# Handing more gathered columns of a graph network's edge passes to ScalarE, VectorE, SyncE and TensorE

## What is computed

```python
# a convolution layer
h = x @ W
msg = h[src] * norm[:, None]
out = segment_sum(msg, dst, num_segments=n_nodes)
# an edge convolution: theta, phi and a maximum
msg = (x[src] - x[dst]) @ tw.T + tb + phi[dst]
agg = segment_max(msg, dst, num_segments=n_nodes)
```

## Time and profile before

| | us |
|---|---|
| median of three runs | 9439.49 (9435.47 to 9441.98) |
| the profiled execution | 9444.14 |
| its span, first to last instruction | 9442.3 |
| a pass, first to last gather (passes 2 to 7) | 980.4 |
| the first pass | 1009.4 |

### The profile page before, as it was taken

One profiled execution on the slowest core, in us unless ns is written; L12 is line 12 of the kernel. 1 busy time (PEld: TensorE's weight loads), 2 busy tenths in 40 slices (PEclk: granted clock), 3 DMA queues, 4 the chain that ended last, 5 costly groups with the idle time before them and its releaser, 6 DMA issues. The chain is left out here.

```text
span 9442.3 us, 137452 instructions
## 1 busy us (share of the span) xinstructions
PE 1819.4 (19%) x9607; PEld 1531.1 (16%) x9607; DVE 3654.1 (39%) x20408; ACT 3485.0 (37%) x23810; POOL 6987.7 (74%) x6815
## 2 busy tenths in 40 slices
PE   2000057788884000020002000020002000020000
PEld 1000046777774000010001000010001000010000
DVE  4333344444443333333333333333334333333333
ACT  4444221111114444334442444334442444324441
POOL 5777668888883777777777777777776777777777
PEclk6555567777777555565556555565555555555555
DMA  6444535555553333333333333333334333333333
GB/s 214 161 159 158 190 79 77 77 77 77 75 72 111 108 108 112 110 108 108 113 111 111 111 109 108 113 105 112 108 110 138 103 117 111 109 108 110 108 112 128
DMA packets 483882, 1071.04 MB, mean 113 GB/s; under 512 B 162484, under 2 KB 293278, under 8 KB 428104
## 3 DMA queue, kind: packets, MB, share of 16 engines
q0 software_dynamic: 310432, 442.95, 21.5%
q1 hardware_dynamic: 169557, 619.06, 17.8%
q10 hardware_dynamic: 2940, 1.00, 0.1%
HBM read 511.83 MB, written 559.14 MB: 113 GB/s over the span
## 5 line engine op out<-in xcount | busy, mean ns | idle before, releaser
L1035 POOL DMA_INDIRECT WORK<-table,S x5502 | 5194.3, 944 | 1923.2 <-issue 1689.0
L1071 DVE COPY FE<-XF 128x4 uint8 x9856 | 1311.1, 190 | 3271.9 <-issue 1824.8
L1114 ACT COPY FE<-XF 128x4 uint8 x20608 | 2101.3, 191 | 1104.6 <-issue 1092.0
L1134 ACT COPY WORK<-psum 128x512 f32<-128x512 f32 (+1 forms) x1456 | 846.3, 581 | 2874.1 <-DVE psum L1089 2864.6
L1304 POOL DMA_INDIRECT acc<-TOT,stage x832 | 1301.3, 1564 | 274.6 <-issue 209.7
L1089 DVE SCALAR_TENSOR_TENSOR psum<-psum,RESET,WORK 128x128 f32<-128x128 f32 x3320 | 1189.1, 358 | 493.3 <-DMA WORK<-table,S 426.8
L1154 PE MATMUL psum<-ident,FE 128*128 128x128 f32 x238 | 106.5, 447 | 6110.0 <-ACT FE L1114 4714.0
L1089 DVE SCALAR_TENSOR_TENSOR psum<-psum,KEEP,WORK 128x128 f32<-128x128 f32 x2490 | 896.9, 360 | 639.9 <-DMA WORK<-table,S 278.8
L1154 PEld LDWEIGHTS psum<-ident,FE 128*128 128x128 f32 x238 | 43.3, 182 | 6172.5 <-issue 5903.0
L1438 ACT COPY TOT<-psum 128x512 f32<-128x512 f32 x208 | 121.9, 586 | 1250.2 <-DMA acc<-TOT,stage 1245.0
L1509 DVE SCALAR_TENSOR_TENSOR BASE<-psum,WEIGHT,BASE 128x128 f32<-128x128 f32 x832 | 234.1, 344 | 761.9 <-PE psum L1379 761.8
(11 more groups left out here) (255 smaller groups left out, 2540.4 us busy)
## 6 DMA issues: line engine op xcount, KB each, us to landing
run_rows<-WORK SPq DMA_DIRECT2D x357, 1024.0 KB, 4.2
WORK<-table SPq DMA_DIRECT2D x10752, 0.5 KB
WORK<-table,S POOLq DMA_INDIRECT x5502, 2.6
fill_rows<-BASE SPq DMA_DIRECT2D x52, 1024.0 KB, 6.8
WORK<-fill_rows SPq DMA_DIRECT2D x104, 512.0 KB, 3.7
table<-TF SPq DMA_DIRECT2D x56, 384.0 KB
WORK<-carry_rows SPq DMA_DIRECT2D x49, 384.0 KB, 6.6
acc<-TOT,stage POOLq DMA_INDIRECT x832, 3.3
```

The lines of the kernel that those rows point to most:

```text
L1035: pool.indirect_dma_start(RING_T[:, b * WIDE + k, :], None, table, table_row(table, INDEX[:, t:t + 1]))\
L1071: i = dve.tensor_copy(PICKED[:, s, e:e + 1].bitcast(u8), TT[:, ds(held_rows["dve"][e % 32], 4)])
L1114: i = act.copy(PICKED[:, j % 2, e:e + 1].bitcast(u8), TT[:, ds(held_rows["act"][e % 32], 4)])
L1134: act.copy(RING_T[:, t % SPAN:t % SPAN + n, :], CHAINED[:, t % PSUM_COLS:t % PSUM_COLS + n, :])\
```

## The change

46 columns of AWAY become 81: ScalarE 23 to 30, VectorE 11 to 24, SyncE 12 to 15, and TensorE, which brought none, 12. Copies are made in units of 32 edges, one register load each (UNIT, four units to a column). ScalarE does a unit at five of every eight groups of four columns, ahead of the lift; VectorE a unit at every other group; TensorE a unit at every fourth. TensorE's copy is a matmul with the identity as weights and one column of XF as moving data, into PSUM bank 7, which ScalarE copies to PICKED when all 128 edges are there (`drawn`). Tiles are turned three groups ahead of use in banks 5 and 6 and copied to the ring two groups ahead. The chain of running values has 20 columns of PSUM instead of 24. SyncE fetches the second to last column of every third (once in sixteen blocks: fourth) block: a half after store c-3 and one after store c-2, where it no longer waits for the store just issued. XF is read back after block 50. The place numbers for ROWB are made by 12 strided operations instead of 46.

```diff
-PSUM_COLS = 24
-BY_ACT = [t for t in range(60, 772, 32)]
-BY_DVE = [t for t in range(108, 772, 64)]
-BY_SP = [t for t in range(84, 800, 64)]
-EDGES = 16
-X_BLOCK = 48
-STEP_EDGES = 2
+PSUM_COLS = 20
+UNIT = 32
+UNITS = P // UNIT
+TT_LAST = 800
+ACT_QUADS = [q for q in range(TT_LAST // QUAD) if q % 8 in (0, 1, 3, 4, 6)]
+BY_ACT = [t for t in (QUAD * (q + 5) for q in ACT_QUADS[UNITS - 1::UNITS]) if t < TT_LAST]
+DVE_STEPS = list(range(4, TT_LAST, 8))
+BY_DVE = [t for t in (QUAD * (s // QUAD + 5) + 1 for s in DVE_STEPS[UNITS - 1::UNITS]) if t < TT_LAST]
+PE_QUADS = list(range(1, TT_LAST // QUAD, 4))
+BY_PE = [t for t in (QUAD * (q + 6) + 3 for q in PE_QUADS[UNITS - 1::UNITS]) if t < TT_LAST]
+SP_BLOCKS = [c for c in range(3, TT_LAST // WIDE) if c % 16 in (3, 6, 9, 12, 0)]
+BY_SP = [WIDE * c + WIDE - 2 for c in SP_BLOCKS]
+X_BLOCK = 50
...
                 def pick_edges(t):
+                    if t not in DVE_STEPS:
+                        return
+                    j, unit = divmod(DVE_STEPS.index(t), UNITS)
...
+                    if unit == 0:
+                        wait(dve, tt_copied, len(tt_quads) if j == 0 else 0)
+                        wait(dve, off_turned, FROM_TT.index(BY_DVE[j - 2]) + 1 if j > 1 else 0)
+                    rows = row_offsets(mybir.EngineType.DVE, len(BY_ACT) + j, unit)
+                    for e in range(UNIT):
+                        i = dve.tensor_copy(PICKED[:, 2 + j % 2, unit * UNIT + e:unit * UNIT + e + 1].bitcast(u8),
+                                            TT[:, ds(rows[e], 4)])
...
                 for q in range(quads):
                     pick_edges(q)
+                    for j, col in enumerate(BY_PE):
+                        if q == col // QUAD - 4:
+                            act.wait_ge(built_p, j + 1)
+                            wait(act, off_turned, FROM_TT.index(BY_PE[j - 2]) + 1 if j > 1 else 0)
+                            act.copy(PICKED[:, 4 + j % 2, :], bank(7)[:, 0:P]).then_inc(drawn, 1)
...
+                    rows = row_offsets(mybir.EngineType.PE, len(BY_ACT) + len(BY_DVE) + j, unit, 1)
+                    for e in range(UNIT):
+                        m = nc.tensor.matmul(bank(7)[:, unit * UNIT + e:unit * UNIT + e + 1], ident[:],
+                                             XF[:, ds(rows[e], 1)], start=True, stop=True)
...
+                for q in range(quads):
+                    for j, col in enumerate(FROM_TT):
+                        if q == col // QUAD - 3:
+                            turn(j, col)
+                    pick_edges(q)
...
                 def fetch(after):
                     for j, col in enumerate(BY_SP):
                         c = col // WIDE
-                        k = after - max(c - RING, -1)
-                        parts_of = ((0, 64), (64, 64)) if c >= RING else ((0, 128),)
-                        if not 0 <= k < len(parts_of):
+                        half = after - (c - RING + 1)
+                        if half not in (0, 1):
                             continue
...
+                        wait(sp, stored[c % RING], c // RING * 16 if half == 0 else 0)
+                        for unit in range(half * UNITS // 2, (half + 1) * UNITS // 2):
+                            rows = row_offsets(mybir.EngineType.SP, len(AWAY) - len(BY_SP) + j, unit, 4 * F)
+                            for e in range(UNIT):
+                                p = unit * UNIT + e
+                                sp.dma_start(RING_T[p:p + 1, col % SPAN, :].bitcast(u8),
+                                             flat_table[:, ds(rows[e], 4 * F)]).then_inc(fetched[j % 2], 16)
...
-                fetch(-1)
```

More of the change, by code:

```diff
@@ L632, in _ @@
                                   ALU.is_equal).then_inc(hot, 1)
-                for k, (t, size) in enumerate([(t, 4) for t in BY_ACT + BY_DVE] + [(t, 4 * F) for t in BY_SP]):
-                    i = dve.tensor_single_scalar(AWAY_F[:, k:k + 1], SRCF[:, t:t + 1], float(size), ALU.mult)
+                k = 0
+                for cols_of, period, size in ((BY_ACT, 5, 4), (BY_DVE, 1, 4), (BY_PE, 1, 1), (BY_SP, 5, 4 * F)):
+                    n = len(cols_of)
+                    for r in range(period):
+                        own = cols_of[r::period]
+                        assert own == list(range(own[0], own[-1] + 1, own[1] - own[0]))
+                        i = dve.tensor_single_scalar(AWAY_F[:, k + r:k + n:period],
+                                                     SRCF[:, own[0]:own[-1] + 1:own[1] - own[0]],
+                                                     float(size), ALU.mult)
+                    k += n
                 i.then_inc(hot, 1)
@@ L995, in _, with row_offsets @@
                 wait(sp, x_parked, 16 * NG if x_loads == 1 else 0)
-        def row_offsets(engine, k, first, n, size=4):
+        def row_offsets(engine, k, unit, size=4):
             return nc.values_load_multi_w_load_instructions(
-                ROWB[k:k + 1, first:first + n], engines=[engine], min_val=0, max_val=(N_PAD - 1) * size,
+                ROWB[k:k + 1, unit * UNIT:(unit + 1) * UNIT], engines=[engine], min_val=0,
+                max_val=(N_PAD - 1) * size,
                 skip_runtime_bounds_check_because="the offsets are made of node numbers below N_PAD")[1]
@@ L1059, in pick_edges @@
                 def pick_edges(t):
[L1060 to L1074, removed]
+                    if t not in DVE_STEPS:
+                        return
+                    j, unit = divmod(DVE_STEPS.index(t), UNITS)
+                    if j >= len(BY_DVE):
+                        return
+                    if unit == 0:
[5 more added lines that the diff above has]
+                                            TT[:, ds(rows[e], 4)])
+                    if unit == UNITS - 1:
+                        i.then_inc(built_v, 1)
                 for t in range(T):
@@ L1104, in pick_edges @@
                 def pick_edges(q):
[L1105 to L1117, removed]
+                    if q not in ACT_QUADS:
+                        return
+                    j, unit = divmod(ACT_QUADS.index(q), UNITS)
+                    if j >= len(BY_ACT):
+                        return
+                    if unit == 0:
+                        wait(act, off_turned, FROM_TT.index(BY_ACT[j - 2]) + 1 if j > 1 else 0)
+                    rows = row_offsets(mybir.EngineType.Activation, j, unit)
+                    for e in range(UNIT):
+                        i = act.copy(PICKED[:, j % 2, unit * UNIT + e:unit * UNIT + e + 1].bitcast(u8),
+                                     TT[:, ds(rows[e], 4)])
+                    if unit == UNITS - 1:
+                        i.then_inc(built_a, 1)
                 for q, (t, n) in enumerate(tt_quads):
@@ L1143, in pe_part, with pick_edges, turn @@
                 wait(pe, tt_copied, len(tt_quads))
-                for j, col in enumerate(FROM_TT):
+                def pick_edges(q):
+                    if q not in PE_QUADS:
+                        return
+                    j, unit = divmod(PE_QUADS.index(q), UNITS)
+                    if j >= len(BY_PE):
+                        return
+                    if unit == 0:
+                        wait(pe, drawn, j)
+                    rows = row_offsets(mybir.EngineType.PE, len(BY_ACT) + len(BY_DVE) + j, unit, 1)
+                    for e in range(UNIT):
+                        m = nc.tensor.matmul(bank(7)[:, unit * UNIT + e:unit * UNIT + e + 1], ident[:],
+                                             XF[:, ds(rows[e], 1)], start=True, stop=True)
+                    if unit == UNITS - 1:
+                        m.then_inc(built_p, 1)
+                def turn(j, col):
                     wait(pe, homed, j - 1)
@@ L1153, in pe_part @@
                         pe.wait_ge(built_v, k + 1)
-                    nc.tensor.transpose(bank(6 + j % 2)[:, 0:P], PICKED[:, s, :], ident[:]).then_inc(off_turned, 1)
+                    else:
+                        k = BY_PE.index(col)
+                        s = 4 + k % 2
+                        pe.wait_ge(drawn, k + 1)
+                    nc.tensor.transpose(bank(5 + j % 2)[:, 0:P], PICKED[:, s, :], ident[:]).then_inc(off_turned, 1)
+                for q in range(quads):
[3 more added lines that the diff above has]
+                    pick_edges(q)
                 pe.wait_ge(reduced, T)
```

20 lines of the change are left out of this document (7 added, 13 removed).

## The result

The changed kernel takes 9680.35 us (9677.33 to 9683.28), the kernel before 9438.62 us beside it (9435.47 to 9441.98). The ratio is 1.0256, with a 95% interval of 1.0238 to 1.0274: **slower by 242 us**. The forecast was 9635, range 9475 to 9955. The profiled execution of after has a span of 9681.5 us.

The account below looks back on a forecast made before the run. SyncE's fetch loop, 59.2 us for three blocks against GpSimd's 53.9, was to bound the kernel. 9444 + 94 (six passes) + 97 (first pass) + 5 (X read back) = 9640, the median 4.7 lower: 9635 us, range 9475 to 9955.

Parts of the forecast that it names:

- The bound changes from GpSimd to SyncE's loop: SyncE's fetch from store to store takes 59.2 us for three blocks, where GpSimd needs 53.9; +15.6 us a pass.
- Two halves of 27.8 us: SyncE's fetch: each half of 64 rows behind a store, with two register loads, takes 27.8 us; 55.6 for both.
- The end, 2.9 + 0.7 us: After SyncE's last row: 1.0 until usable, VectorE 1.2, lift and store 0.7; another 0.7 for VectorE work not hidden.
- ScalarE and TensorE, set at 0: ScalarE's 36 of 39 us and TensorE's 18 of 19 us at most are hidden: 0; far end +19 a pass.
- the start: From a pass's first gather to its first store: 33 us, against 27.4 before.
- free blocks: Three blocks a pass with no fetched column behind them, at VectorE's own speed: 18.5 us each, 20 in the first pass.
- The price of TensorE's copy: TensorE's unit of 32 matmuls: 0.25 us each from transposes, so 8 us, 16 at twice that; a load of 2.
- The first pass: With zeroing of 1 MB ahead of each store, loop 66 us (61.2 to 68); +97 us (+28 to +131).
- +4.1 for late fetches: First pass: a late fetch puts the next fetch's first load behind 4 MB of zeroing and stores, +4.1 us a loop.
- X read back: Reading X back beside a pass's last 16 columns, three times, holds VectorE 0 to 11 us each: +5 us.
- GpSimd stays the bound: Rival: no store slows the halves' first loads, fetch 51.6, loop 54.5: 9138 us or some 60 more; 10% with the page's rule.
- VectorE becomes the bound: Rival: one of VectorE's two loads a block meets a store, a block takes 19.9 to 22.3 us: 9955 us; 17%.

Follow-up runs that it names:

- experiment 1: The changed kernel without SyncE's 15 fetched columns, which GpSimd gathers instead (766 gathers a pass): 9268.95 us.
- experiment 3: The changed kernel with SyncE's first register load of each half fetch issued ahead of the preceding store instead of behind it: 9473.49 us.
- 4: The changed kernel with the second register load of each half fetch done twice, so three loads a half: 10082.52 us; a first form (9686.33 us) was void.
- experiment 2: The changed kernel without VectorE's 24 columns, which GpSimd gathers instead (775 gathers a pass): 9540.48 us.
- experiment 8: Changed kernel with 12 SyncE columns, 32 rows after each store, loads ahead of stores, one ScalarE unit moved: 9522.77 us; same without TensorE's columns: 9524.04 us.
- experiment 9: The version fetching 32 rows after each store, with TensorE's columns, and VectorE's units moved from columns 4 and 12 of a block to 0 and 10: 9315.6 us.

## Why the prediction was right

**The bound changes from GpSimd to SyncE's loop: right.** With SyncE's columns gone and 20 gathers a pass fewer than before, the time is 171 us under the kernel before, and 140 gathers at 1.249 us are 175 (experiment 1); loads taken out of SyncE's chain or put into it move the time in their sense (3, 4).

**Two halves of 27.8 us: right**, 55.6 measured. The load behind a store is the slow kind, as the earlier trace rows had it.

**The end, 2.9 + 0.7 us: too short.** It is 4.0. The term that was mis-sized is ScalarE and TensorE, set at 0. I had judged them by their mean load (36 of 39 us; 8 to 16 of 19 us) and they do fit on the mean. But the lift that ends a loop stands behind one particular unit or one particular home copy in ScalarE's queue, and that behind up to 128 matmuls in TensorE's, which come in bursts after a wait. The mean said nothing on that place. VectorE's units have a share in it: without them (experiment 2), as with a longer chain (4), no end is late. How the 0.4 us divides among the three engines stays open. With the loop 0.44 longer, 15 loops are +6.6; the start +0.8, free blocks +1.0, the last gather behind store 48 +0.6: 9 us a pass, +54 in six.

The price of TensorE's copy was too low, too. I had taken 0.25 us an edge from transposes, 8 us a unit, and 16 as the far end. The transposes have one matmul each in the trace and the edges two: 0.43 us an edge and 13.7 us a unit. With its load of 2.2 that is 16 of the 19 us between two units, so TensorE fits on the mean, but close to the far end.

**The first pass: loop 64.7 instead of 66.** Both halves took what the earlier trace rows had for one, 30.9 and 30.4 us: the first load of a half took 3.8 to 6.2 us there, mostly over 5, and not the 8 that +4.1 for late fetches implied: 15 x 1.3 = 19 us less. The start took 1.3 more and the free blocks 23.6 each instead of 20, 11 more. Together 8 us under the forecast.

**X read back: +2.6 us with all else outside the passes**, instead of +5.

The errors are +54, -8 and -2 us, 44 in all; the forecast was 45 us short.

**The rivals.** *GpSimd stays the bound* was to come if the first load of each half met no store, with a fetch of 51.6 us and a loop of 54.5. Experiment 3 made the fetch 52.1, and the loop was 57.6 still, for TensorE and the moved load were next: that rival's sum had the same gap in the end term. *VectorE becomes the bound* wasn't the case here (of the 78 loads of VectorE between blocks 5 and 45 of the fourth pass, 11 met a store), and its mechanism is real: experiments 8 and 9 made it and undid it.

## What to carry to other kernels

Where one engine's transfers stand between two of its own stores, write down the loop from store to store and compare it with the time its blocks have; a tenth over (59.6 us against 53.9) is the whole loss, however idle that engine looks. Cover judged by an engine's mean load says nothing of the one instruction that the path needs next: look up what stands ahead of it in that in-order queue. And place small register loads away from the large stores that their own engine's progress sets off, for the two come together in every round.

## What the runs showed of the hardware

A register load of 32 words takes twice as long when it meets the issue of a 1 MB store: on VectorE 4.09 against 2.13 us (experiment 8, the slow ones issued from 0.2 us ahead of the store to 0.3 us behind it), on SyncE 4.0 against 2.15, and mostly 5.1 to 6.2 us in the first pass, where a zeroing of 1 MB goes with each store. ScalarE and TensorE show it in fewer loads: 4.0 us in five and 4.3 in two of the changed kernel's fourth pass, against 2.06 and 2.27. Issued 2.8 us after the store, VectorE's loads take 2.2 to 2.9 us, 2.5 at the median (experiment 9).

SyncE issues 32 rows in 10.2 to 10.8 us behind a load, but in 10.9 to 12.0 us right behind a store (experiment 3).

TensorE's copy of an edge, a matmul in float32 with one moving column and an address from a register, stands as two matmuls in the trace (3072 for 1536 edges) and took 0.43 us, at the clock given below.

TensorE was busy 693 of 1006 us in the fourth pass, against 25 of 982 in the fifth pass before, and its granted clock was 0.50 in both, the lower of its two levels, 1.2 GHz. Stretch, busy us (instructions) of PE, PEld, DVE, ACT, POOL, granted clock, DMA share, GB/s, before and after:

```profile
6221.00:7203.00 982.00, 25.48 (x83) 13.28 (x83) 358.32 (x2238) 419.78 (x3197) 741.98 (x786) 0.50 0.35 112
5287.00:6293.00 1006.00, 693.46 (x3187) 675.78 (x3187) 626.26 (x3902) 519.42 (x4137) 708.23 (x751) 0.50 0.33 105
```
